# A graph attention loop: VectorE's small operations of a group spread between its large ones, the group's own logits in two halves, its weighing four chunks later, a fifth buffer of gathered rows

## What is computed

```
def gat_layer(x, src, dst, W, att_src, att_dst, bias):   # N = 6250 nodes, H = 4 heads, F = 64
    n = x.shape[0]
    h = (x @ W).reshape(n, H, F)
    a_src = jnp.sum(h * att_src[None], axis=-1)
    a_dst = jnp.sum(h * att_dst[None], axis=-1)
    e = jax.nn.leaky_relu(a_src[src] + a_dst[dst], 0.2)
    m = jax.ops.segment_max(e, dst, num_segments=n)
    ...
    ex = jnp.exp(e - m[dst])
    denom = jax.ops.segment_sum(ex, dst, num_segments=n)
    alpha = ex / (denom[dst] + 1e-16)
    msg = h[src] * alpha[..., None]
    out = jax.ops.segment_sum(msg, dst, num_segments=n)
    return out.reshape(n, H * F) + bias

```

## Time and profile before

| | us |
|---|---|
| median of 3 runs | 7773.34 (7767.19 to 7786.14) |
| span of the profiled execution, all that there is of it | 8769.9 |
| attention sweep in it: first gather to last addition | 7238.6 to 8594.4 |
| PE, DVE, ACT, POOL busy over the span | 73%, 55%, 28%, 58% |
| the same from 7300 to 8500 | 84%, 82%, 68%, 61% |

### The profile page before, as it was taken

How to read it: one execution, slowest core, us unless ns; L and a number is a source line. 1 busy time by engine, 2 the same in 40 slices (tenths; PEclk the granted TensorE clock), 3 DMA queues, 4 the chain that set the end, 5 groups by cost and what they waited for, 6 DMA issues and landing times.

```text
span 8769.9 us, 105363 instructions
## 1 busy us (share of the span) xinstructions
PE 6380.8 (73%) x25864; PEld 4099.8 (47%) x25864; DVE 4844.9 (55%) x16703; ACT 2445.7 (28%) x7538; POOL 5049.1 (58%) x5303
## 2 busy tenths in 40 slices
PE   8977777789677876777776555556777776888881
PEld 4544555544455554444443333334444444666651
DVE  7974545554344443344443444434555557888888
ACT  4631111122011111111112222211222225666665
POOL 4656666600666665666665666656665545666650
PEclk9987878799789888888887767767898888999995
DMA  1013333344444444444456666663333335666662
GB/s 52 3 45 115 90 91 90 90 109 154 116 136 136 136 136 110 133 137 136 137 132 190 214 210 211 216 166 90 88 88 86 87 72 177 192 194 192 194 188 70
DMA packets 559179, 1141.73 MB, mean 130 GB/s; under 512 B 111895, under 2 KB 304380, under 8 KB 558462
## 3 DMA queue, kind: packets, MB, share of 16 engines
q0 software_dynamic: 249024, 659.51, 28.6%
q1 hardware_dynamic: 195886, 366.27, 12.0%
q10 hardware_dynamic: 113680, 109.21, 3.7%
HBM read 822.31 MB, written 312.26 MB: 129 GB/s over the span
## 4 chain that ended last, share of the span: by engine, by line
PE 40%; another core or an unknown queue 21%; DVE 16%; issue 14%; ACT 4%; DMA 1%; DVEq 1%; ACTq 1%; SPq 0%; POOL 0%; POOLq 0%
PE ps L1109 11%; PE ps L1331 6%; PE ps L1301 4%; PE ps L1519 4%; DVE AY L1783 3%; PE ps L1463 2%; PE ps L1506 2%; DVE edges L1650 2%; PE ps L1497 2%; PE ps L1492 2%; PE ps L1464 1%; PE ps L1098 1%; DVE AY L2069 1%; DVE edges L1649 1%
## 5 line engine op out<-in xcount | busy, mean ns | idle before, releaser
L1783 DVE TENSOR_TENSOR AY<-AY,ps 128x256 f32 (+1 forms) x4160 | 1744.1, 419 | 3173.0 <-remote 1681.1
L719 POOL DMA_INDIRECT g<-rel_d,edges x2496 | 2365.8, 948 | 1690.1 <-issue 672.4
L1109 PE MATMUL ps<-g,rows 128*128 128x256 f32 (+1 forms) x4160 | 1327.6, 440 | 278.7 <-DVE AY L1783 113.0
L1109 PE MATMUL ps<-g,oh 128*128 128x256 f32 (+1 forms) x4160 | 1373.7, 448 | 133.7 <-DVE oh L1766 35.7
L1109 PEld LDWEIGHTS ps<-g,rows 128*128 128x128 f32 x4160 | 835.4, 220 | 636.0 <-issue 381.6
L719 POOL DMA_INDIRECT g<-rows_d,edges x832 | 804.6, 967 | 544.4 <-issue 209.1
L719 POOL DMA_INDIRECT g<-in_x,edges x832 | 794.0, 954 | 442.0 <-issue 210.7
L1109 PEld LDWEIGHTS ps<-g,oh 128*128 128x128 f32 x4160 | 855.7, 224 | 396.3 <-issue 227.2
L1331 PE MATMUL ps<-AY,turned 128*128 128x512 f32 x1568 | 831.6, 658 | 174.6 <-ACT turned L746 83.9
L2056 DVE TENSOR_REDUCE AY<-ps 128x4 f32<-128x512 f32 x832 | 571.4, 687 | 177.4 <-PE ps L1497 114.0
L746 ACT ACTIVATE wt<-ps 128x512 f32<-128x512 f32 (+1 forms) x448 | 250.0, 559 | 1478.4 <-remote 625.1
(11 more groups left out here) (380 smaller groups left out, 9906.1 us busy)
## 6 DMA issues: line engine op xcount, KB each, us to landing
rel_d<-wt ACTq DMA_DIRECT2D x392, 256.0 KB
turned_d<-AY SPq DMA_DIRECT2D x104, 512.0 KB
wt<-turned_d SPq DMA_DIRECT2D x104, 512.0 KB
AY<-marks_d SPq DMA_DIRECT2D x104, 512.0 KB
rel_d<-g SPq DMA_DIRECT2D x49, 1024.0 KB
g<-rel_d,edges POOLq DMA_INDIRECT x2496
marks_d<-oh SPq DMA_DIRECT2D x104, 256.0 KB
marks_d<-rows SPq DMA_DIRECT2D x104, 256.0 KB
```

What stands on the lines that cost most here:

```text
L719: pool.indirect_dma_start(out=g[:, j, 0:width], out_offset=None, in_=table, in_offset=bass.IndirectOffsetOnAxis(ap=edges[:, word, c:c + 1] ...
L1109: ins = pe.matmul(sum_slot(order, j), one_hot_at(j % OHS), g[:, j, 0:width], start=True, stop=True)
L1783: dve.tensor_tensor(tile_at(A, t, width), tile_at(A, t, width), sum_slot(order, j), ALU.add)\
```

## The change

All of it is in the attention sweep, and the arithmetic stays as it is.

- **DVE.** `lowered` is taken apart into `top_logit` (twice, for the group's last row before and after its maxima; it replaces a copy of the old maximum), `edge_logits`, `max_logits`, `leaky`, `guarded` and `lowered`. Each stands between two large operations, at j = 0, 5, 6 and 7. The eight running maxima of a group come two to a place at j = 4 to 7, one ahead of the addition and one behind it. The load of bucket numbers goes from j = 0 to j = 4. `lg` is doubled, and `red` has eight places for four. DVE waits at j = 4 for `s_dm`, as the maxima written there are read by `own_logits`.
- **PE.** `own_logits` runs in two halves of four products, at j = 2 and j = 3. PE's `logit_rows` goes from j = 6 to j = 4.
- **ACT.** The copy of the own row goes from j = 2 to j = 4, the exponentials from j = 4 to j = 7 and behind the weighing, `logit_parts` from j = 5 to j = 2, ACT's `logit_rows` from j = 7 to j = 5.
- **Distances.** Weighing, weighed sum and addition stand 17, 19 and 20 places behind the spread (13, 15, 16 before), `rescaled` of group k comes in i = k+2 at j = 3, and the loops run one group longer at the end.
- **Buffers.** `GBUF` is 5; the fifth group buffer lies in the parts of `edges` that hold the words 1 to 3, which this sweep does not read. POOL's gather of chunk c waits for the weighed sum of chunk c - 40.
- **SP.** Its order of transfers and its waits are as they were.

```diff
@@ constants
-GBUF = 4
+GBUF = 5
-EX_AT, SC_LAG, MM_LAG, ADD_LAG = 4, 5, 7, 8
+OWN_AT, EX_AT, SC_LAG, MM_LAG, ADD_LAG = 4, 7, 9, 11, 12
+REDS = 8
@@ buffers
+        g_last = edges_f[:, 1:4, :].rearrange("p w c -> p (w c)")[:, 0:GR * W4].rearrange("p (s d) -> p s d", d=W4)
-        lg = Y[:, o3:o3 + (GR + 1) * 2 * H].rearrange("p (s h) -> p s h", h=2 * H)
+        lgs = [Y[:, o3 + k * (GR + 1) * 2 * H:o3 + (k + 1) * (GR + 1) * 2 * H].rearrange("p (s h) -> p s h", h=2 * H)
+               for k in range(2)]
@@ ScalarE
-            for i in range(NGR + 2):
+            for i in range(NGR + 3):
                 k = i - 1
                 for j in range(GR):
                     c = GR * i + j
-                    if j == 2 and 0 <= k < NGR:
+                    if j == 2 and i + 1 < NGR:
+                        logit_parts(i + 1)
+                    if j == OWN_AT and 0 <= k < NGR:
                         act.wait_ge(s_dm, k + 1)
                         if k:
                             act.wait_ge(s_l0, k)
                         copy(own_row.rearrange("p s h -> p (s h)"), ps[:, 6, 0:2 * H * GR]).then_inc(s_own_row, 1)
+                    if j == 5 and i + 1 < NGR:
+                        logit_rows(i + 1)
+                    if 0 <= c - GR - SC_LAG < NCH:
+                        weigh(c - GR - SC_LAG)
                     if j == EX_AT and 0 <= k < NGR:
                         ...
-                    if 0 <= c - GR - SC_LAG < NCH:
-                        weigh(c - GR - SC_LAG)
-                    if j == 5 and i + 1 < NGR:
-                        logit_parts(i + 1)
-                    if j == GR - 1 and i + 1 < NGR:
-                        logit_rows(i + 1)
@@ TensorE
-            def own_logits(k, buckets):
-                pe.wait_ge(s_maxed, GR * (k + 1))
-                if k:
-                    pe.wait_ge(s_own_row, k)
-                for j in range(GR):
+            def own_logits(k, buckets, lo, hi):
+                if lo == 0:
+                    pe.wait_ge(s_maxed, GR * (k + 1))
+                    if k:
+                        pe.wait_ge(s_own_row, k)
+                for j in range(lo, hi):
                     ...
-                ins.then_inc(s_dm, 1)
+                if hi == GR:
+                    ins.then_inc(s_dm, 1)
...
-                    if j == 1 and 0 <= k < NGR:
-                        own_logits(k, buckets)
-                    if j == 6 and i + 1 < NGR:
+                    if j in (2, 3) and 0 <= k < NGR:
+                        own_logits(k, buckets, GR // 2 * (j - 2), GR // 2 * (j - 1))
+                    if j == 4 and i + 1 < NGR:
                         logit_rows(i + 1)
@@ VectorE
-            def lowered(k, t, next_t):
-                ...
+            def top_logit(k, half, t):
+                dve.wait_ge(s_maxed, GR * (k if half == 0 else k + 1))
+                link.begin(dve.tensor_tensor(lgs[k % 2][:, GR, H * half:H * (half + 1)], tile_at(max_l, t, H),
+                                             tile_at(dst_l, t, H), ALU.add))
+            def edge_logits(k):
+                dve.wait_ge(s_own_row, k + 1)
+                link.begin(dve.tensor_tensor(lgs[k % 2][:, 0:GR, 0:H], own_row[:, :, 0:H], group_at(k)[:, :, D:W3], ALU.add))
+            def max_logits(k):
+                dve.tensor_tensor(lgs[k % 2][:, 0:GR, H:2 * H], own_row[:, :, 0:H], own_row[:, :, H:2 * H], ALU.add)\
+                    .then_inc(s_l0, 1)
+            def leaky(k):
+                lg = lgs[k % 2]
                 link.ended()
                 dve.wait_ge(s_l0, k + 1)
                 link.begin(dve.scalar_tensor_tensor(lg, lg, 0.2, lg, ALU.mult, ALU.max))
-                if next_t is not None:
-                    link.begin(dve.tensor_copy(old_m, tile_at(max_l, next_t, H)))
+            def guarded(k):
+                lg = lgs[k % 2]
                 link.ended()
-                link(dve.tensor_tensor(lg[:, :, H:2 * H], lg[:, :, H:2 * H], lg[:, :, 0:H], ALU.max))
+                link.begin(dve.tensor_tensor(lg[:, :, H:2 * H], lg[:, :, H:2 * H], lg[:, :, 0:H], ALU.max))
+            def lowered(k):
+                lg = lgs[k % 2]
+                link.ended()
                 dve.tensor_tensor(lower, lg[:, :, 0:H], lg[:, :, H:2 * H], ALU.subtract).then_inc(s_e, 1)
...
-            for i in range(NGR + 2):
+            for i in range(NGR + 3):
                 k = i - 1
                 for j in range(GR):
                     c = GR * i + j
                     if c < NCH:
                         reduced(c)
-                    if j == 0:
+                    if j == GR // 2:
                         tiles = {n: v for n, v in tiles.items() if n >= i - 2}
                         if i + 1 < NGR:
                             tiles[i + 1] = group_buckets(mybir.EngineType.DVE, i + 1)
+                        if 0 <= k:
+                            dve.wait_ge(s_dm, min(k + 1, NGR))
+                            link.ended()
+                    if j >= GR // 2 and i < NGR:
+                        maxed(GR * i + 2 * j - GR, tiles[i][2 * j - GR])
+                    if 0 <= k < NGR:
+                        if j == 0:
+                            top_logit(k, 1, tiles[k][0])
+                        if j == 5:
+                            edge_logits(k)
+                        if j == 6:
+                            leaky(k)
+                        if j == 7:
+                            lowered(k)
                     late = c - GR - ADD_LAG
                     if 0 <= late < NCH:
                         added(late, tiles[late // GR][late % GR])
-                    if j == 2 and 0 <= k < NGR:
-                        lowered(k, tiles[k][0], tiles[i][0] if i < NGR else None)
-                    if i < NGR:
-                        for m in (0, 1, 2) if j == 2 else (j,) if j > 2 else ():
-                            maxed(GR * i + m, tiles[i][m])
-                    if j == ADD_LAG - 1 and 0 <= k < NGR:
-                        rescaled(k, tiles[k][0])
+                    if j >= GR // 2 and i < NGR:
+                        maxed(GR * i + 2 * j - GR + 1, tiles[i][2 * j - GR + 1])
+                    if 0 <= k < NGR:
+                        if j == 0 and i < NGR:
+                            top_logit(i, 0, tiles[i][0])
+                        if j == 5:
+                            max_logits(k)
+                        if j == 6:
+                            guarded(k)
+                    if j == ADD_LAG - GR - 1 and 0 <= k - 1 < NGR:
+                        rescaled(k - 1, tiles[k - 1][0])
```

32 lines of the change are left out of this document (12 added, 20 removed).

## The result

The changed kernel takes **7746.33 us** (median of 11 runs, 7726.29 to 7768.59) against 7772.84 for the kernel before beside it (11 runs): a ratio of 0.9969 [0.9962, 0.9977], 24 us. It was taken twice more, at 0.9962 [0.995, 0.9973] and 0.9972 [0.9959, 0.9984], 25 and 21 us by the medians. The forecast was 7581.

The account below looks back on a forecast made before the run. The bound was engines waiting for each other. Floors: POOL 10.0, DVE 9.9, PE 9.4, SP's loop 9.8 to 10.7; DVE's 9.9 plus stops and halves gave 10.5 us for 12.48, 192 us less: 7581, range 7530 to 7680.

Parts of the forecast that it names:

- The carry-over: Attention sweep: its 192 us loss in the profile taken over whole to the timed median, 7773 to 7581.
- 1.5 us of stops a group: DVE before the change: idle time beyond its 11.0 us of work in a group of about 12.5 us.
- The bunch of SP: Marks, `miss` and `ohT`, 1.31 MB, go out together before PE's first spread: 5.9 to 6.8 us, up to 7.6.
- SP's loop: Bunch, PE's places j = 0 to 2, next marks: 9.8 us at 5.9, 10.7 at 6.8, 11.5 at 7.6.
- Rival B: SP's bunch takes 6.9 to 8 us, every first spread waits: 11.5 us a group, 7680 us; chance 0.19.
- 9.4 (PE at full clock): PE's need for a group: eight places of 0.93, `own_logits` 1.77, transposition about 0.2; 9.4 us, as before.
- DVE's sum: DVE's need for a group after the change: 9.9 us for 11.0, seven new small operations at 0.08 to 0.15 each.
- PE's halves: `own_logits` in two halves: two places of 1.82 us instead of one of 2.70, leaving DVE 0.1 to 0.3 to wait.
- the slack of ACT: ACT's work is 8.5 us a group; its copy and exponentials come early enough, nothing there is late.
- C: DVE's small operations not hidden, each paying its own duration: 12.4 us a group, no change (7765); chance 0.05, shared with E.
- POOL's floor: POOL's gathers start 1.25 us apart when nothing holds them: 10.0 us a group, never less.
- A: POOL's floor is reached, other stops fall into slack: 10.1 us a group, 7540 us; chance 0.14.

Follow-up runs that it names:

- both_2: Changed kernel with next group's `miss`, `ohT` issued before marks, first spread waiting for `miss` alone: 7641.57 us, 0.983; slower chip (`both`): 8790.32 us, 1.0015.
- The three runs that take the wait away: Changed kernel with `miss` and `ohT` ahead of marks (7662.46 us), with first spread waiting for `miss` alone (7648.26), and with both edits (7641.57).
- the control: Kernel before with the two edits on SP's loads (order and wait) and nothing else: 7773.72 us, 0.9998.
- before_again: Kernel before, unchanged, profiled once more in the conditions of the result: 7774.76 us, span 7772.7.
- block_2: both_2 with `edge_logits`, `max_logits`, `leaky`, `guarded` and `lowered` in one block at j = 7: 7736.08 us, 0.9949 of the kernel before.
- one_piece_both_2: both_2 with `own_logits` in one piece at j = 2 in place of two halves: 7733.13 us, 0.9941 of the kernel before.

## Why the prediction was wrong

The sign was right, the size was not: 21 to 27 us in place of 192. The sweep's own rows split the difference. From first to last `leaky` the forecast had 1292 and 1090 us, 202 less.

| | first to last `leaky`, us | |
|---|---|---|
| forecast, before | 1291.8 |, slower chip |
| before, on the chip timed | 1209.8 | 82 of the 202 never there |
| forecast, after | 1090 | |
| after | 1180.4 | 90 more than forecast |
| both_2 | 1073.8 | 16 less than forecast |

**The carry-over failed first.** The step "the profiled execution is 997 us longer than the median; no row tells where" was answered with a reason ("no reason to be stretched by it"), when it could not be answered: the excess lay also in the stops, the very thing that the sum was to take away. Of the 1.5 us of stops a group, 0.8 were not there on the chip timed. Had the 82 us been taken off, the forecast would have been 7663: inside the range, and half the way to the result.

**The bunch of SP was mis-sized.** The term was right in kind and place: marks, `miss` and `ohT` go out together, PE's first spread waits for the last. It had 5.9 to 6.8 us, "up to 7.6 with some unevenness", and the forecast took its middle, at which SP's loop stays at the other floors. Measured are 6.8 in the median and 7.2 in the mean, with 12 of 90 over 8.2. The loop itself was right: by the prediction's own line it is 10.7 us at 6.8, and the median group is 10.74. What failed is the middle value, and the overlap in "PE is ahead of DVE when the group begins, so 1 us of waiting there costs DVE nothing": the stops of PE are 1.1 us in the median, and DVE stands 1.3 us a group. Rival B had "6.9 to 8 us and a group takes 11.5 us", and a group takes 11.46. B's mechanism is what happened, with the chance of 0.19 that it got, but its figure is partly luck: its loop at the mean of 7.2 gives 11.1, and the rest is the clock, which B had no term for. The three runs that take the wait away give 84 to 105 us back, and the control shows that the same edits bring nothing where the loads are not late.

**The clock had no term.** Against both_2 the changed kernel loses 107 us in its sweep, and about half of that sits in few groups. The median group is 10.74 us against 10.23 in both_2, 0.51 x 103 = 53 us; the mean lies 0.72 above the median against 0.20, another 54 us. Most of this second half are the eight groups of 15.9 to 18.8 us, each with the clock at 1.2 GHz and seven of them behind a stop of PE of 2.7 us or more. Their stops are in it as well; by the pairs compared above, the clock is 4 to 6 us of most of them. The prediction's sum went by "9.4 (PE at full clock)" and its answer to B looked at the wait alone.

**What held.** DVE's sum (small operations at 0.07 to 0.14 between large ones, so C is out), PE's halves (1.82 us from spread to spread), the slack of ACT, POOL's floor (783 instructions in 1000 us in both_2 are 1.28 us apart, just above the 1.25 of the earlier trace rows, so A may be next; that was not tried), and 10.5 us a group as soon as the loads are in time: 10.43. Spreading five of the eight small operations is worth 95 us with all else in place, some 42 of it by the clock, and the halves 88 to 91. The two don't add up, since all of the change with the edits is worth 129 us over before: with either one undone PE and DVE stop each other again, and the kernel is back near 7735. How much of the 129 hangs on the fifth buffer and the later weighing was not tried on the faster chip.

## What to carry to other kernels

Before a difference of a profile is taken over to a timed median, the two must agree on the unchanged kernel; where they don't, the stops are the first thing to distrust: here DVE was busy for 10.25 us a group in both profiles of the kernel before, and beyond the 11.0 us of its sum a group took 1.5 us in one and 0.7 in the other. When a step moves, list each queue that its semaphore releases, put the loads on a queue in the order of their deadlines, and wait only for the load that the next instruction reads: here that was worth 84 to 105 us beside the change's 24. A wait that an engine can afford by its slack can still cost the clock of TensorE, so a long stop of PE is dearer than its length.

## What the runs showed of the hardware

Chips of one kind ran the same program in 7771 to 7776 and in 8781 to 8806 us, with granted clocks over the span of 0.915 in before_again and 0.844 in the first profile. In the slower profiles DVE's reductions stand for up to 1.8 us (the first) and 2.9 us (both) after the matmul that they wait for has ended by its row. TensorE's clock went to 1.2 GHz behind stops of very different length: for 9 to 14 us behind 2.7 to 3.5 us in the changed kernel and for 7 us behind 0.9 in block_2, while other stops of the same lengths were followed by the full clock (3 of 10 stops of over 2.5 us in the changed kernel, 64 of 77 of 0.8 to 1.1 us in block_2). In one_piece_both_2 it went down for 3 us 23 times with no stop of over 0.4 us beside it, only one of 0.4 to 0.5 us some 7 us earlier. What decides is open. A stretch of 7 us at the low clock cost a group 2.8 us in block_2, one of 10 to 14 us cost 4.5 to 6 in the changed kernel. A 4-element operation of DVE between large ones moves the next start by 0.07 us, one of 36 elements by 0.10 and one of 72 by 0.14, where the old ones in a row stood 0.38 apart. Three transfers of 1.31 MB issued within 1.3 us, beside gathers, took 6.8 us in the median till PE could use the last, and up to 9.2, once 12.8.
